# The first block's token maxima tile by tile on VectorE, and three moves in the queue of TensorE

## What is computed

```python
def act_quant(x):
    scale = 127.0 / jnp.clip(jnp.max(jnp.abs(x), axis=-1, keepdims=True), 1e-05)
    return jnp.clip(jnp.round(x * scale), -128, 127) / scale

h = bit_linear(x, w1)                      # 256 -> 1024
h = depthwise_conv1d(h.transpose(0, 2, 1), conv_w, conv_b).transpose(0, 2, 1)
h = jax.nn.silu(h)
return bit_linear(h, w2)                   # act_quant(h) times w2, 1024 -> 256

def step(h, inp):                          # the scan, in the fourth block
    dt_t, xv_t, B_t, C_t = inp
    h = jnp.exp(dt_t[:, :, None] * A[None]) * h + (dt_t * xv_t)[:, :, None] * B_t[:, None, :]
    return (h, jnp.einsum('bdn,bn->bd', h, C_t))
```

## Time and profile before

| | |
|---|---|
| median of three runs | 2438.21 us (2436.58 to 2440.09) |
| profiled execution | 2443.21 us, span 2441.4 us |
| mean granted clock of TensorE | 0.957 of full speed |
| busy: TensorE, VectorE | 2060.5 us (84%), 1997.9 us (82%) |
| busy: ScalarE, GpSimd | 1507.8 us (62%), 1144.2 us (47%) |
| one turn | about 597 us |

### The profile page before, as it was taken

How to read it: one execution, slowest core, us unless ns; L and a number is a source line. 1 busy time by engine, 2 the same in 40 slices (tenths; PEclk the granted TensorE clock), 3 DMA queues, 4 the chain that set the end, 5 groups by cost and what they waited for, 6 DMA issues and landing times.

```text
span 2441.4 us, 26347 instructions
## 1 busy us (share of the span) xinstructions
PE 2060.5 (84%) x9096; PEld 1153.2 (47%) x9096; DVE 1997.9 (82%) x2422; ACT 1507.8 (62%) x2395; POOL 1144.2 (47%) x562
## 2 busy tenths in 40 slices
PE   4998878898899887889789988888978988888886
PEld 2236664345424665434542466543543256644444
DVE  7865879996985678998797577899788748799977
ACT  3664478774376547876547645787464655577844
POOL 2111249992322116997222122799532302389942
PEclk8999999999999998999999999899999999989998
DMA  6200000000220000000031000000003100000000
GB/s 215 89 1 1 18 1 1 1 1 1 86 63 1 1 18 1 0 1 1 1 109 40 1 1 18 0 1 0 1 14 109 27 1 1 1 0 1 1 1 18
DMA packets 41074, 51.29 MB, mean 21 GB/s; under 512 B 9072, under 2 KB 32368, under 8 KB 40944
## 3 DMA queue, kind: packets, MB, share of 16 engines
q1 hardware_dynamic: 40944, 49.62, 6.3%
HBM read 26.25 MB, written 10.49 MB: 15 GB/s over the span
## 4 chain that ended last, share of the span: by engine, by line
DVE 40%; PE 35%; ACT 11%; issue 8%; POOL 4%; DMA 1%; SPq 0%; DVEq 0%; ACTq 0%; POOLq 0%
DVE big L2208 17%; PE psum L835 10%; ACT big L1317 5%; PE psum L983 5%; ACT mid L1317 5%; PE psum L971 3%; PE psum L956 3%; PE psum L1175 3%; DVE mid L1809 2%; PE psum L990 2%; PE psum L1208 2%; POOL big L2359 2%; DVE negmax L1908 2%; PE psum L900 2%; DVE mid L2099 1%
## 5 line engine op out<-in xcount | busy, mean ns | idle before, releaser
L1317 ACT ACTIVATE big<-psum 128x512 f32<-128x512 f32 (+2 forms) x604 | 457.0, 775 | 275.5 <-PE psum L971 146.0
L2359 POOL TENSOR_TENSOR big<-big 128x2048 f32<-128x2048 f32 x124 | 561.8, 4531 | 39.4 <-DVE big L2208 38.9
L1175 PE MATMUL psum<-big,ident 128*128 128x512 f32 x992 | 506.2, 616 | 65.6 <-POOL big L2359 65.6
L2208 DVE TENSOR_TENSOR_SCAN big<-psum,b,big 128x512 f32<-128x512 f32 x404 | 489.6, 1263 | 8.3 <-ACT psum L1317 8.2
L1908 DVE TENSOR_REDUCE negmax<-psum 128x1 f32<-128x512 f32 x512 | 318.6, 678 | 35.2 <-PE psum L956 34.1
L1317 ACT ACTIVATE psum<-mid,aneg 128x512 f32<-128x512 f32 x404 | 268.5, 680 | 81.0 <-DVE big L2208 80.9
L1175 PEld LDWEIGHTS psum<-big,ident 128*128 128x128 f32 x992 | 173.9, 193 | 230.9 <-POOL big L2359 141.9
L956 PE MATMUL psum<-mid 96*128 96x512 bf16 x512 | 187.1, 385 | 26.5 <-DVE negmax L1908 12.8
L971 PE MATMUL psum<-mid 98*128 98x512 bf16 x512 | 182.0, 382 | 15.8 <-ACT big L1317 12.1
L1317 ACT ACTIVATE mid<-mid 128x513 f32<-128x513 f32 (+3 forms) x120 | 105.8, 886 | 116.9 <-DVE mid L1778 115.4
L2141 DVE TENSOR_TENSOR big<-mid,psum 128x1024 f32<-128x1024 f32 (+1 forms) x128 | 157.3, 1229 | 15.5 <-PE psum L1146 15.5
(11 more groups left out here) (235 smaller groups left out, 3896.3 us busy)
## 6 DMA issues: line engine op xcount, KB each, us to landing
mid<-big SPq DMA_DIRECT2D x192, 64.0 KB, 2.6
mid<-scratch SPq DMA_DIRECT2D x192, 64.0 KB, 2.2
scratch<-big SPq DMA_DIRECT2D x4, 1536.0 KB, 6.3
out<-hres SPq DMA_DIRECT2D x8, 513.0 KB, 3.8
onorm<-in_x SPq DMA_DIRECT2D x8, 512.0 KB, 4.3
big<-in_w SPq DMA_DIRECT2D x2, 1024.0 KB, 6.3
big<-in_wg SPq DMA_DIRECT2D x1, 1024.0 KB, 9.6
big<-in_wu SPq DMA_DIRECT2D x1, 1024.0 KB, 11.6
```

Source lines behind the costliest of these rows:

```text
L1175: mm = nc.tensor.matmul(y_psum[:, c], ident[:, :], st(1, k)[:, c], start=(n == 0), stop=(n == NS - 1))
L1317: return nc.scalar.activation(o, a, func, **kw)
L2208: V.tensor_tensor_scan(st(0, k)[:, c], decays(DT * k + c), bx, b0[:, p, n, c:c + 1], ALU.mult, ALU.add).then_inc(scanned, 1)
L2359: G.tensor_tensor(st(1, k), st(0, k), c_row(k).unsqueeze(1).broadcast_to([P, DT, S]), ALU.mult).then_inc(hc_ready, 1)
```

## The change

In the first block ScalarE now writes the absolute value of each tile (signal f_abs) and VectorE takes the running maximum (f_max); `half_max_of` is gone. The loop on VectorE is three steps longer, and the maxima of the second image stand ahead of the first image's scales. In `down_project` the order of the two groups for the second image is turned round in the first block. At the start of the scan b(0) is spread ahead of the last z tile, c(0) no longer waits for wy0, b(1) follows at once, and the product of y0 goes to the last bank of y_psum instead of c_psum, behind both.

```diff
                         else:
-                            pe.wait_ge(absmax_part, q_of(q, p))
+                            pe.wait_ge(*((f_max, (HT - 1) * (p + 1)) if q == 1 else (absmax_part, q_of(q // 2, p))))
...
-                        for n, tiles in enumerate(parts_of[::-1] if p else parts_of):
+                        for n, tiles in enumerate(parts_of[::-1] if f and p else parts_of):
...
+                for name, p in IN_ORDER:
+                    if (name, p) == IN_ORDER[-1]:
+                        spread_b(0)
+                    inputs(name, p)
...
                 def spread_c(k):
                     if k:
                         pe.wait_ge(c_copied, k)
                     else:
-                        pe.wait_ge(w_first, 1)
+                        pe.wait_ge(z_silu, DT * PAIR)
...
+                    elif k == 0 and c == DT - 1:
+                        pe.wait_ge(w_first, 1)
...
-                    pe.wait_ge(z_silu, DT * PAIR)
                     pe.wait_ge(first_state, PAIR + 6)
                     for c in range(KT):
                         for k in range(DT):
-                            mm = nc.tensor.matmul(c_psum[:, PAIR * c:PAIR * c + PAIR], wout[:, k, c * P:(c + 1) * P],
+                            mm = nc.tensor.matmul(y_psum[:, DT - 1, PAIR * c:PAIR * c + PAIR], wout[:, k, c * P:(c + 1) * P],
...
-                spread_b(0)
+                spread_c(0)
+                spread_b(1)
                 project_first()
-                spread_b(1)
-                spread_c(0)
...
-                for s in range(PAIR * HT + 5):
+                for s in range(PAIR * HT + 6):
...
+                    p, c = divmod(s - 6, HT)
+                    if 0 <= p < PAIR:
+
+                        act.wait_ge(f_silu, HT * p + c + 1)
+                        if c >= 3:
+                            act.wait_ge(f_max, (HT - 1) * p + c - 2)
+                        run(mid1(p, 4 + c % 2) if c else mid1(p, 6), big8(p, 1)[:, c], ACT.Abs).then_inc(f_abs, 1)
...
                                 if k == 0:
                                     copy_b(0)
-                                    act.wait_ge(w_first_full, 1)
-                                    run(wy0[:, :], c_psum[:, 0:PAIR * KT], ACT.Copy).then_inc(w_first, 1)
...
+                            if k == 0 and c == DT - 1:
+                                act.wait_ge(w_first_full, 1)
+                                run(wy0[:, :], y_psum[:, DT - 1, 0:PAIR * KT], ACT.Copy).then_inc(w_first, 1)
...
-                def half_max_of(p, n):
-
-                    V.tensor_reduce(mid1(p, (6, 7)[n]), big8(p, 1)[:, 4 * n:4 * n + 4].rearrange("p c t -> p t c"), AX_X,
-                                    ALU.max, apply_absolute_value=True).then_inc(half_max, 1)
...
-                def running_max(p, c):
-
-                    dve.wait_ge(prod_abs, HT * p + c + 1)
+                def running_max(p, c, absolute, done):
+
+                    dve.wait_ge(absolute, HT * p + c + 1)
...
-                for s in range(PAIR * HT + 4):
+                for s in range(PAIR * HT + 7):
...
-                    if s == HT + 2:
-                        dve.wait_ge(f_silu, 4)
-                        half_max_of(0, 0)
-                    if s == HT + 5:
-                        dve.wait_ge(f_silu, HT)
-                        half_max_of(0, 1)
+                    p, c = divmod(s - 7, HT)
+                    if 0 <= p < PAIR and c:
+                        running_max(p, c, f_abs, f_max)
                 scales(1, 0)
-                dve.wait_ge(f_silu, HT + 4)
-                half_max_of(1, 0)
-                dve.wait_ge(f_silu, HT * PAIR)
-                half_max_of(1, 1)
                 scale_tiles(1, 0)
```

More of the change, by code:

```diff
@@ L593, in build @@
         prod_max = signal("prod_max")
-        half_max = signal("half_max")
+        f_abs = signal("f_abs")
+        f_max = signal("f_max")
         taps_ready = signal("taps_ready")
@@ L1137, in turn_products @@
                 mm.then_inc(full[FILLS["first", 0][0]], 1)
-                for name, p in IN_ORDER:
-                    inputs(name, p)
-                pe.wait_ge(bc_split, 6 * PAIR)
                 def spread_row(k, r, o):
@@ L1805, in absmax @@
                                     apply_absolute_value=True).then_inc(absmax_part, 1)
-                def half_max_of(p, n):
-                    V.tensor_reduce(mid1(p, (6, 7)[n]), big8(p, 1)[:, 4 * n:4 * n + 4].rearrange("p c t -> p t c"), AX_X,
-                                    ALU.max, apply_absolute_value=True).then_inc(half_max, 1)
-                    if n:
-                        dve.wait_ge(half_max, 2 * p + 2)
-                        V.tensor_tensor(mid1(p, 6), mid1(p, 6), mid1(p, 7), ALU.max).then_inc(absmax_part, 1)
-                def running_max(p, c):
-                    dve.wait_ge(prod_abs, HT * p + c + 1)
+                def running_max(p, c, absolute, done):
+                    dve.wait_ge(absolute, HT * p + c + 1)
                     if c > 1:
-                        dve.wait_ge(prod_max, (HT - 1) * p + c - 1)
-                    V.tensor_tensor(mid1(p, 6), mid1(p, 6), mid1(p, 4 + c % 2), ALU.max).then_inc(prod_max, 1)
+                        dve.wait_ge(done, (HT - 1) * p + c - 1)
+                    V.tensor_tensor(mid1(p, 6), mid1(p, 6), mid1(p, 4 + c % 2), ALU.max).then_inc(done, 1)
                 def scales(q, p):
@@ L2246, in turn_vectors @@
                     if 0 <= p < PAIR and c:
-                        running_max(p, c)
+                        running_max(p, c, prod_abs, prod_max)
                 scale_tiles(3, 0)
```

## The result

| | before | changed |
|---|---|---|
| median, five runs each | 2440.06 us | 2427.19 us |
| lowest to highest | 2436.58 to 2442.23 | 2424.85 to 2429.42 |
| profiled execution | 2443.21 us | 2428.13 us |
| granted clock of TensorE, mean | 0.957 | 0.961 |

The changed kernel takes 0.995 of the time of before, 95% interval 0.9937 to 0.9964: 12.9 us less. The forecast was 2427.5. That the two numbers all but coincide is chance: by the interval the gain lies between 8.8 and 15.4 us. The steps behind the forecast came true in part only.

The account below looks back on a forecast made before the run. VectorE held 40% of the chain, TensorE 35%. Scan start 5.7 plus maxima and w2 order 5 took 10.7 off the profiled 2443.2, giving 2432.5; that execution being 5.0 above the median, forecast 2427.5 us, range 2414 to 2440.

Parts of the forecast that it names:

- Part 1: Scan start: b(1) ready earlier, VectorE and GpSimd move up, 0.3 us in the first turn, 1.8 in three: 5.7 us.
- Part 2: Convolution stage: running maxima replace reductions; VectorE's count falls 7.5 us per turn, yet about 2 us per turn is lost.
- First: Convolution stage: ScalarE's 9.3 us free barely fits 15 absolute values of 9.4 us; its copies come later by tenths.
- Second: First image's maxima: three of seven start within a GpSimd product of 1.1 us and are blocked, adding 3.3 us.
- Third: First scales, behind the second image's maxima, come 4.9 us late; TensorE idles 4 us, low clock; second scales 1.4 late.
- Fourth: GpSimd's first-image product starts with VectorE's, takes 5.6 us; second-image products start about 1483.0 instead of 1480.91 and 1481.08.
- GpSimd's first three-tile product over 5 us: Sign that the forecast is right: GpSimd's first-image product in the convolution stage, 3.09 us before, lasts over 5 us.
- The slow rival: GpSimd takes each image's pair first, VectorE's product stands 3.1 us behind it; 2438 to 2445 us, chance 0.08.
- Part 3: Second image's w2: 20 of 32 matmuls go ahead, leaving 12 behind ScalarE, 1.4 us at full clock.
- deduction of 2 for the low clock: Last w2 group: low clock costs 1.5 us in one or two turns, lowering the 7.0 at full clock to 5.

Follow-up runs that it names:

- e3: Kernel before with the new scan start and the new order of w2's halves, old maxima kept: 2420.85 us, ratio 0.9926.
- e2: Kernel before with only the new order of w2's two matmul groups for the second image: 2424.20 us, ratio 0.9940.
- e1: Kernel before with only the new scan start, b(0), c(0) and b(1) spread earlier: 2435.81 us, ratio 0.9989.
- e4: Kernel before with only the running maxima from ScalarE's absolute values: 2444.93 us, ratio 1.0032.
- e12: Kernel before with only the 16 absolute values per turn added on ScalarE, read by nobody, reductions kept: 2438.43 us, ratio 0.9999.
- e5: Kernel before with new scan start and w2 order, running maxima for the second image only, first scales ahead of its last five: 2420.74 us, ratio 0.9925.
- e6: Changed kernel with the first image's scales ahead of the last three maxima of the second image: 2415.33 us, ratio 0.9896.
- e7: Changed kernel with 26 filler matmuls instead of 10 ahead of the first image's row matmuls: 2421.30 us, ratio 0.9933.
- e10: e6 with GpSimd's first three-tile product behind VectorE's, and ScalarE's second-image row copies ahead of its first-image roundings: 2407.85 us, ratio 0.9869.

## Why the prediction was right, and where not

**Part 1: right at the first products, and not to be counted on behind them.** Predicted 5.7, measured 3.1 alone (interval 0.5 to 4.9) and 3.4 as the difference of e3 and e2. The terms at the first products were right: no idle time ahead of b(1), second product 4.28 us after the first scan, 0.2 gained in the first turn, 1.9 to 2.1 in the others. The cost of b(0)'s matmul, "nothing to 0.2", was 0.2 in each turn. Wrong was "The steps behind them wait only for each other, so all of them move along": VectorE's fourth tile also waits for TensorE, and at the low clock 2.2 us went there in e1. In the profiled execution of the changed kernel nothing was lost, 6.4 less 0.8 us, because the clock was higher in two turns. The sum had no term for this, so it is luck that its 5.7 is met there.

**Part 2: right in sign and nearly in size.** Predicted about 2 us per turn lost where VectorE's count falls by 7.5; e4 lost 6.0 in time, 8.2 in stage.
*First*, ScalarE has room: shown by e12.
*Second*, blocked maxima: shown. In the third turn the pair at 1443.96 and the one at 1449.65 took 2.0 us more than they do alone, where 3.3 was predicted, and the last maximum came 0.6 us before the predicted 1469.2 in old time. The Trainium skill (SBUF — State Buffer, "Who interferes with whom") says that a reduction never contends with GpSimd, and that an instruction with two inputs in SBUF does; e5 and the earlier trace rows show both sides, 3.1 us lost by five maxima beside a product that left two reductions at 7.3.
*Third*, late scales and low clock: shown by e6 and e7. Its size was off: I took 4.09 us for the twenty row matmuls and it was 5.11 in every turn; ten of them are on the way to the row copy. VectorE's scaling started at 1464.29, 1473.3 in old time, against 1473.2 predicted, since the maxima ended 0.6 earlier.
*Fourth*: the step that failed. "Now it starts with VectorE's product on the same row; where they met before, at 1481.08, it took 5.61" put GpSimd behind VectorE. Before, the second image's pair had not started together: GpSimd came 0.17 us later. Here both wait for one signal and GpSimd was 0.02 us ahead, four times out of four. So VectorE's product lasted 5.74, GpSimd was done by 1467.35, ScalarE's roundings no longer held the row copy, and the slip went to the second scales instead: 1469.96, or 1479.0, against 1478.0. Two errors met: the rounding ended at 1483.3 in old time and not at 1482.4, while both second products started at 1483.3 and 1483.5, near the 1483.0 predicted. The sign "GpSimd's first three-tile product over 5 us" did not come: 3.08. The slow rival had this mechanism, at a chance of 0.08, and the mechanism came in every turn. It did not decide, because the second image's pair did not meet in the same way.

**Part 3: right.** Alone 14.7 us; the prediction's 5 for parts 2 and 3 with a loss of 8 in part 2 implies 13. The 12 matmuls ran at full clock in all four turns (1.49), where I had expected the low clock in one or two. Parts 2 and 3 together gave 4.7 in stage; 5 was predicted. For the full clock the prediction's own sum was 7.0, so that the 5 was met is partly luck: its deduction of 2 for the low clock was not needed, and the work ahead of the last group came that much later than predicted.

**Sum.** 5 and 5.7 were predicted; the traces hold 4.7 and 5.4 (5.6 by the third product with c), and the parts alone 8.7 (14.7 less 6.0) and 3.1. The forecast's 10.7 stands beside 12.9 measured, within what two medians can tell.

## What to carry to other kernels

Before an operation is exchanged for a cheaper one, look at what stands beside it on the other engine: here 0.6 us maxima replaced reductions that nothing disturbs, and lost their gain to one 3.1 us product. When code is merged into a loop, ask what it now stands ahead of: moving the first image's scales back was worth as much as the whole change. And a gain at the start of a pipelined loop counts only once its first full period has been read too, in every turn and beside the granted clock.

## What was not expected of the hardware

- An instruction of VectorE on 5 elements per partition, one input in SBUF and a constant, took 2.27 us instead of 0.17 while GpSimd ran a product (e10), as long as that product lasted. The rounding of 2565 elements to bf16, also with one input, took 2.83 with and without GpSimd beside it. The rounding of 1026 elements, of the same kind, was held up: alone it took 0.69 to 0.70 us, and 1.47 each of the seven times that it met a GpSimd product of 2.08 us (four in the kernel before, three in the changed one). It also works at another rate, 0.68 ns per element against 1.10 for the 2565. The Trainium skill (SBUF — State Buffer, "Who interferes with whom") says that such an instruction can contend, when it runs in a mode that uses both of VectorE's ports; the trace agrees in the 1026 elements, faster per element and held up, and in the 2565, slower and not. For the five elements the trace shows the wait and not the mode.
  In the kernel before, third turn, VectorE and then GpSimd:

```profile
1442.34 1.47 DVE L1707 TENSOR_SCALAR mid<-mid 128x1026 bf16<-128x1026 f32 x1
1441.18 2.08 POOL L2321 TENSOR_TENSOR big<-big,mid 128x513 f32<-128x513 f32 x1 [5.40 <-ACT big L1317]
```

- Two instructions that one signal releases: GpSimd began 0.02 to 0.03 us ahead of VectorE in all four turns, and VectorE's was the one held up: 5.74 us instead of 2.83, beside a product of 3.08.
- Twenty row matmuls behind the same 1.42 us of idle time took 2.86 us in some turns and 3.74 in others (e6, e10): how long TensorE idled just before does not settle the clock by itself. The same holds for 2.69 us in e7 (5.11 and 2.86), and for 4.21 us in e4, where the twenty took 4.41 and 4.48 in two turns and 5.11 in two. The Trainium skill (TensorE: Matmul & The Clock Gate, "HAM oscillation — how this bites in real kernels") tells of a loop in which the clock falls at each of its long waits; the trace agrees for the wait of 4.21 us, where the clock was 0.50 behind it in all four turns of the changed kernel. The wait of 1.42 us is shorter than those that it tells of.
